# Attention rounds of the loop take 48 places instead of 64

## The reference, cut to what matters

```python
M = Bc * Nc                                     # 16384 nodes
h = (x_flat @ W_gat).reshape(M, HEADS, NUM_EXPERTS)
src = jnp.concatenate([edge_index[0], loops])   # 524288 edges, then one loop per node
dst = jnp.concatenate([edge_index[1], loops])
e = leaky_relu(a_src[src] + a_dst[dst], negative_slope=0.2)
e_max = jax.ops.segment_max(e, dst, num_segments=M)
ee = jnp.exp(e - e_max[dst])
denom = jax.ops.segment_sum(ee, dst, num_segments=M)
msg = h[src] * (ee / (denom[dst] + 1e-16))[:, :, None]
agg = jax.ops.segment_sum(msg, dst, num_segments=M)
...
'edge_index': jax.random.randint(ks[6], (2, N_EDGES), 0, B * N, jnp.int32)   # B * N = 32768
```

## Time and profile before

| what | value |
|---|---|
| median of 3 runs | 4333.23 us (4332.97 to 4335.96) |
| the profiled execution's own time | 4334.45 us |
| its span in the trace | 4332.5 us |
| busy: TensorE, VectorE, ScalarE, GpSimd | 68%, 70%, 36%, 31% |
| attention stage | about 2419 to 4140 us |
| turns in it | 20 (1280 gathers of L1481 at 64 a turn) |

### The profile page before, as it was taken

The page is one execution under the profiler, slowest core; times in us unless marked ns, Lnnn a source line. Parts: engine busy times, 40 slices in busy tenths (PEclk is TensorE's granted clock), DMA queues, the critical chain, the costliest instruction groups (busy, mean ns, idle before and its releaser), DMA issues. The chain is left out here.

```text
span 4332.5 us, 30277 instructions
## 1 busy us (share of the span) xinstructions
PE 2940.0 (68%) x9220; PEld 1488.6 (34%) x9220; DVE 3027.5 (70%) x4723; ACT 1553.3 (36%) x2238; POOL 1345.7 (31%) x1414
## 2 busy tenths in 40 slices
PE   6888897999999998998657235545554553554019
PEld 2333343343444443433234122322232332322019
DVE  8999668787888786987664546655654664665575
ACT  2222235444445454445453123323222322332117
POOL 0000000000000000001111577777777777777600
PEclk8888998999999999999768567666776776776559
DMA  4211322454545454548556212111111211111237
GB/s 152 76 64 54 112 93 79 128 176 140 174 150 172 141 179 139 187 143 272 168 178 225 33 29 51 37 37 44 47 37 44 47 37 40 31 18 18 23 134 287
DMA packets 341083, 454.19 MB, mean 105 GB/s; under 512 B 82749, under 2 KB 256712, under 8 KB 332090
## 3 DMA queue, kind: packets, MB, share of 16 engines
q1 hardware_dynamic: 289290, 389.20, 27.8%
q0 software_dynamic: 51632, 63.07, 7.7%
HBM read 340.70 MB, written 111.42 MB: 104 GB/s over the span
## 5 line engine op out<-in xcount | busy, mean ns | idle before, releaser
L1481 POOL DMA_INDIRECT got<-scratch_tab,src_at x1280 | 1224.0, 956 | 390.3 <-issue 378.7
L687 PE MATMUL in_ps<-tokens,w_in 128*128 128x512 f32 x2048 | 937.1, 610 | 4.4 <-issue 4.4
L1435 PE MATMUL hid_ps<-tokens,w 128*128 128x512 f32 x512 | 321.7, 762 | 823.0 <-ACT hid L1663 800.9
L614 POOL MEMSET tokens<- 1x128 int32 x1 | 0.2, 195 | 1923.0 <-DVE tokens L1069 1923.0
L687 PEld LDWEIGHTS in_ps<-tokens,w_in 128*128 128x128 f32 x2048 | 393.7, 196 | 484.8 <-issue 484.8
L704 PE MATMUL out_ps<-w_out,act 128*128 128x512 f32 x1024 | 478.8, 611 | 1.7 <-DMA w_out<-in_m_WoutT 1.7
L1068 DVE TENSOR_TENSOR tokens<-tokens 128x1024 f32<-128x1024 f32 x380 | 465.0, 1224 | 9.1 <-ACT tokens L852 8.0
L1069 DVE TENSOR_TENSOR tokens<-tokens 128x1024 f32<-128x1024 f32 x380 | 464.6, 1223 | 0.0
L1435 PEld LDWEIGHTS hid_ps<-tokens,w 128*128 128x128 f32 x512 | 111.4, 241 | 919.4 <-ACT hid L1663 810.7
L1588 DVE TENSOR_TENSOR hold<-by_value,is_loop 128x256 f32<-128x256 f32 x20 | 8.5, 426 | 581.7 <-ACT by_value L1674 581.7
L1674 ACT ACTIVATE by_value<-got 128x1536 f32<-128x1536 f32 x20 | 80.5, 4027 | 733.5 <-DMA got<-scratch_tab,src_at 733.5
(11 more groups left out here) (270 smaller groups left out, 4086.3 us busy)
## 6 DMA issues: line engine op xcount, KB each, us to landing
w_out<-in_m_WoutT SPq DMA_DIRECT2D x256, 512.0 KB, 4.6
w_in<-in_m_WinT SPq DMA_DIRECT2D x128, 512.0 KB, 4.0
scratch_y<-ys SPq DMA_DIRECT2D x25, 1024.0 KB, 4.0
got<-scratch_tab,src_at POOLq DMA_INDIRECT x1280, 2.4
tokens<-scratch_xt SPq DMA_DIRECT2D x8, 2048.0 KB, 9.4
scratch_sz<-zst SPq DMA_DIRECT2D x64, 256.0 KB, 5.0
gz<-scratch_sz SPq DMA_DIRECT2D x64, 256.0 KB, 5.0
tokens<-scratch_y SPq DMA_DIRECT2D x16, 1024.0 KB, 8.4
```

The source lines that it names most:

```text
L687: last = t_.matmul(in_ps[:, z, :], w_in[:, n % WIN, k, :], xT[:, s % 2, k, :], start=(k == 0), stop=(k == KC - 1))
L1435: last = t.matmul(hid_ps[:, f], w1[:, e, f * P:(f + 1) * P], tokens[:, g * QW:(g + 1) * QW], start=True, stop=True)
L1481: g.indirect_dma_start(got[:, y, t, :], None, tab_d[:, :], bass.IndirectOffsetOnAxis(ap=src_at[:, y, t:t + 1], axis=0))\
```

## The change

In the turns of the loop (18 and 19, and more if lists are longer) a turn takes FD = 48 places. The tiles stay 64 wide, and so do all of VectorE's and ScalarE's operations on them; the places 48 to 63 are marked as edges without effect. The carried state is read from column 48 there, at the end of `compute` rather than at the start of the next. The number of rounds of the loop is computed for 96 places a round. Three tiles that were written first by the moved copies are cleared once by GpSimd.

```diff
@@ -46,6 +46,9 @@
 FR = 64
 LOG_FR = 6
 LOG_2FR = 7
+FD = 48
+LOG_GROUP = 5
+THIRD = 21846
 ROW = H16 + 2 * HEADS
 TR = 256
 SUMS = HEADS * (EXP + 1)
@@ -1300,11 +1303,12 @@
                         ck(v.tensor_tensor(len_f[:, 1], ends[:, 2 * P:3 * P], ends[:, P:2 * P], ALU.subtract))
                         ck(v.tensor_scalar(len_f[:, 1], len_f[:, 1], float(-P), None, ALU.add))
                         ck(v.tensor_reduce(len_max, len_f.rearrange("x o p -> x (o p)"), AX.X, ALU.max))
-                        ck(v.tensor_scalar(slots_i, len_max, float(P + 1 + 2 * FR - 1), None, ALU.add))
-                        ck(v.tensor_scalar(slots_i, slots_i, LOG_2FR, None, ALU.logical_shift_right))
-                        ck(v.tensor_copy(len_max, slots_i))
-                        ck(v.tensor_scalar(rounds_i[:], len_max, float(PAIRS + 1), float(PAIRS), ALU.max,
-                                           ALU.subtract))
+                        ck(v.tensor_scalar(len_max, len_max, float(2 * FD - 1 + P + 1 - 2 * FR * PAIRS), float(2 * FD),
+                                           ALU.add, ALU.max))
+                        ck(v.tensor_copy(slots_i, len_max))
+                        ck(v.tensor_scalar(slots_i, slots_i, LOG_GROUP, None, ALU.logical_shift_right))
+                        ck(v.tensor_scalar(slots_i, slots_i, THIRD, None, ALU.mult))
+                        ck(v.tensor_scalar(rounds_i[:], slots_i, 16, None, ALU.logical_shift_right))
                         v.sem_inc(s_rnd, 1)
                         v.wait_ge(s_tw, 48)
                         for n in range(2):
@@ -1402,7 +1406,7 @@
 
 
             def rounds(eng):
-                return eng.value_load(rounds_i[0:1, 0:1], min_val=1, max_val=((NE + P + 2 * FR) >> LOG_2FR) - PAIRS)
+                return eng.value_load(rounds_i[0:1, 0:1], min_val=1, max_val=(NE + P + 2 * FD) // (2 * FD))
 
             @block.sync
             def _(sp):
@@ -1476,8 +1480,8 @@
                     g.indirect_dma_start(b_k[:, y], None, sorted_d[:, :],
                                          bass.IndirectOffsetOnAxis(ap=b_at[:, 0:1], axis=0)).then_inc(s_last, 16)
 
-                def gather(y):
-                    for t in range(FR):
+                def gather(y, n):
+                    for t in range(n):
                         g.indirect_dma_start(got[:, y, t, :], None, tab_d[:, :],
                                              bass.IndirectOffsetOnAxis(ap=src_at[:, y, t:t + 1], axis=0))\
                             .then_inc(s_got[y], 16)
@@ -1494,6 +1498,9 @@
                 g.memset(a_dst[:], 0.0)
                 g.memset(sink[:], -BIG)
                 g.memset(peak[:], 0.0)
+                g.memset(logit[:], 0.0)
+                g.memset(add[:], 0.0)
+                g.memset(hold1[:], 0.0)
                 g.memset(one_f[:], 1.0)
                 g.memset(run[:], 0.0)
                 g.memset(sums[:, 1], 0.0).then_inc(s_block, 1)
@@ -1507,7 +1514,7 @@
                         load_keys()
                         if not first:
                             load_last(1 - y)
-                        gather(y)
+                        gather(y, FR if first else FD)
                         g.wait_ge(s_block, 1)
                         g.sem_clear(s_block)
                         append(1 - y)
@@ -1523,7 +1530,7 @@
 
             @block.vector
             def _(v):
-                def merge(ck, r, y, last_on):
+                def merge(ck, r, y, last_on, width):
 
                     v.wait_ge(s_key, 16 * r + 16)
                     v.tensor_copy(lo_at[:, y], next_lo[:])
@@ -1542,9 +1549,11 @@
                     merged = merge_k[LOG_FR % 2][:].bitcast(I32)
                     v.tensor_scalar(src_at[:, y], merged, M - 1, None, ALU.bitwise_and)
                     ck(v.tensor_scalar(edge_i[:], merged, LOG_M, 1, ALU.logical_shift_right, ALU.bitwise_and))
-                    ck(v.tensor_copy(is_edge[:, y], edge_i[:]))
-                    ck(v.tensor_reduce(n_edge[:], is_edge[:, y], AX.X, ALU.add))
-                    v.tensor_scalar(next_lo[:], next_lo[:], n_edge[:, 0:1], float(FR), ALU.subtract, ALU.add)
+                    if width < FR:
+                        v.memset(is_edge[:, y, width:FR], 1.0)
+                    ck(v.tensor_copy(is_edge[:, y, 0:width], edge_i[:, 0:width]))
+                    ck(v.tensor_reduce(n_edge[:], is_edge[:, y, 0:width], AX.X, ALU.add))
+                    v.tensor_scalar(next_lo[:], next_lo[:], n_edge[:, 0:1], float(width), ALU.subtract, ALU.add)
                     ck(v.tensor_tensor(row_pos[:], row_pos[:], n_edge[:], ALU.add))
                     ck(v.tensor_copy(key_at[:], row_pos[:]))
                     if last_on:
@@ -1565,14 +1574,11 @@
                 def spread(x, n):
                     return x.unsqueeze(1).to_broadcast([P, n, FR])
 
-                def compute(ck, y):
+                def compute(ck, y, n):
 
                     row = by_value[:]
                     v.tensor_scalar(is_loop[:], is_edge[:, y], -1.0, 1.0, ALU.mult, ALU.add)
                     v.tensor_copy(hold0[:, :, 1:F1], spread(is_edge[:, y], HEADS))
-                    v.tensor_copy(logit[:, :, 0:1], peak[:, :, FR:F1])
-                    v.tensor_copy(add_r[:, :, 0:1], run[:, 0:SUMS, FR:F1])
-                    v.tensor_copy(hold1[:, :, 0:1], a_dst[:, :, FR:F1])
                     ck(v.tensor_tensor_scan(dist_f[:], one_f[:], is_edge[:, y], 0.0, ALU.mult, ALU.add))
                     v.tensor_scalar(sink[:, :, 1:F1], spread(is_loop[:], HEADS), -BIG, None, ALU.mult)
                     ck(v.tensor_tensor(dist[:], dist_f[:], is_loop[:], ALU.mult))
@@ -1613,13 +1619,16 @@
                                              .to_broadcast([P, OUTS, FR - d]), run[:, :, d:FR]), wait_apart)
                     ck(v.tensor_scalar(out_at[:, y], lo_at[:, y], bin_f[:, 0:1], sum_cap[:, 0:1], ALU.add, ALU.min))
                     v.sem_inc(s_packed, 1)
+                    v.tensor_copy(logit[:, :, 0:1], peak[:, :, n:n + 1])
+                    v.tensor_copy(add_r[:, :, 0:1], run[:, 0:SUMS, n:n + 1])
+                    ck(v.tensor_copy(hold1[:, :, 0:1], a_dst[:, :, n:n + 1]))
 
                 v.memset(keep_ps[:], 0.0)
                 v.wait_ge(s_gc, 1)
                 ck = Chain(v, s_mch)
                 v.tensor_copy(out_at[:, 1], sum_cap[:])
                 ck(v.tensor_copy(next_lo[:], bin_f[:]))
-                merge(ck, 0, 0, 0)
+                merge(ck, 0, 0, 0, FR)
                 v.wait_ge(s_last, 16)
                 v.wait_ge(s_gc, 2)
                 ck(v.tensor_scalar(b_mark, b_node[:], KEY_LAST, LAST_KEY, ALU.logical_shift_left, ALU.bitwise_or))
@@ -1630,13 +1639,14 @@
                     ck = Chain(v, s_mch)
                     for y in range(2):
                         if first:
-                            merge(ck, r + y + 1, 1 - y, FIRST_LAST if r + y + 1 == 2 * PAIRS else 0)
+                            turn = r + y + 1 == 2 * PAIRS
+                            merge(ck, r + y + 1, 1 - y, FIRST_LAST if turn else 0, FD if turn else FR)
                             count(ck, b_first[:, (r + y + 1) * FR:(r + y + 2) * FR])
                         else:
                             v.wait_ge(s_last, 16 * (r + y + 1) - 16 * (2 * PAIRS - 1))
-                            merge(ck, r + y + 1, 1 - y, FR)
+                            merge(ck, r + y + 1, 1 - y, FR, FD)
                             count(ck, b_k[:, 1 - y])
-                        compute(ck, y)
+                        compute(ck, y, FR if first else FD)
                     v.sem_clear(s_mch)
 
                 for i in range(PAIRS):
@@ -1667,10 +1677,10 @@
                 s.wait_ge(s_mw, 96)
                 s.wait_ge(s_gc, 2)
 
-                def pair(i, work=()):
+                def pair(i, work=(), got_before=0):
                     for y in range(2):
                         mine = list(work[y]) if work else []
-                        wait_apart(s, (s_got[y], 16 * FR * i + 16 * FR))
+                        wait_apart(s, (s_got[y], 16 * FR * i + 16 * FR if work else 16 * FD * i + got_before))
                         s.activation(by_value[:], got[:, y].rearrange("p f x -> p x f"), ACT.Copy).then_inc(s_turned, 1)
                         for n in mine[0:1]:
                             expert(n)
@@ -1700,7 +1710,7 @@
                     pair(i, [range(share[r], share[r + 1]) for r in (2 * i, 2 * i + 1)])
                 outcome(NQ_ALL * EXP - 1)
                 with s.Fori(0, rounds(s)) as i:
-                    pair(i + PAIRS)
+                    pair(i + PAIRS, (), 16 * FR * PAIRS + 16 * FD - 16 * FD * PAIRS)
 
 
         stage.close()
```

## The result

The changed kernel takes 4294.91 us, the median of 6 runs (4293.75 to 4297.71), against 4333.32 us for the kernel before in 6 runs: ratio 0.9909, 95% interval 0.9896 to 0.9922. The forecast was 4295 us, within 4291 to 4299. The execution that was profiled has a span of 4293.6 us.

The account below looks back on a forecast made before the run. GpSimd's issue of gathers, 1.25 us each, was taken to bound the attention stage. 4334.45 - 40.0 (gathers) + 1.5 (memsets) + 0.1 (count of rounds) = 4296.05, median 1.2 lower: 4295 us, range 4291 to 4299.

Parts of the forecast that it names:

- The number of turns: Attention stage's loop: longest list 1102 edges, below the 1120 that would need two rounds, so one round, turns 18 and 19.
- Gathers: Turns 18 and 19: 32 of 1280 gathers go, 16 a turn at 1.25 us, all on the path: 40.0 us less.
- Cover in turns 18 and 19: Time to spare behind GpSimd's gathers: ScalarE 6.8 us and VectorE 10.2 in turn 18, VectorE 9.0 in turn 19.
- another engine takes over: Rival, chance 0.05: VectorE's chain outgrows its 9.0 us cover in the last turn; 4300 us with 5 us beyond it.
- Memsets: Attention stage's start: GpSimd's three new clears hold VectorE's first merge operation, delaying all turns by 1.5 us (bounds 0 to 1.65).
- no hold: Rival, chance 0.22: at the stage's start the added clears cost nothing and gathers start where they did; 4293.3 us.
- Sum: Whole kernel: profiled 4334.45 us with all terms gives 4296.05; the runs' median lies 1.2 below, so 4294.8, say 4295 us.
- the way from the last gather to the next stage, 41.96 us, moves as a block: End of turn 19 to the next stage: tiles stay 64 wide, so nothing in the 41.96 us gets shorter; cost 0.

Follow-up runs that it names:

- the second pair of traces: Both kernels run again unaltered: the changed kernel 4297.09 us beside 4333.54 (ratio 0.9916); the kernel before, one run, 4333.87 us.

## Why the prediction was right

**The number of turns**: right; 1248 gathers and one round.

**Gathers**: right and of the right size, 20.1 us in each turn. That GpSimd's issue sets the length of a turn, on a chip with the usual time and at 48 places and more, was shown both ways, by 32 fewer and by 32 more.

**Cover in turns 18 and 19**: right. VectorE's predicted 9.0 us to spare in turn 19 were 9.33 and 8.21 in two traces, its 10.2 in turn 18 were 10.39 and 10.30. ScalarE's 6.8 were 10.5 and 6.6, since its expert work ends earlier in some executions. The rival that another engine takes over is refuted at 48 places, where all this cover was left over, and true at 40 and at 32 gathers, which go beyond it.

**Memsets**: right; +1.5 was predicted, the longer hold is 1.70 and the first gather 1.64 us later. The rival "no hold" is refuted. The Trainium skill's rule in "SBUF — State Buffer", section "SBUF: two separate sides" (of GpSimd's operations and certain kinds of VectorE's, the first to start on the shared port pair keeps it for its whole instruction, the other fully blocks), gives the direction; the trace goes beyond it. VectorE's operation started at 2422.30, beside the end of the clear of `run`, and was let in only behind the two clears of `sums` that followed, not behind the one that it met.

**Sum**: right within 0.1 us, and that closeness is luck. The step that failed is "the way from the last gather to the next stage, 41.96 us, moves as a block". It grew by 3.5 us: 2.86 through the DRAIN, which the change made longer, and 0.67 through the landing of the last gathers, which the second pair of traces does not repeat (3.4 and 3.5 us). In two sets of runs the changed kernel came 38.4 and 36.5 us below the kernel before beside it, where the terms as measured give -40.2 + 1.6 + 2.9 = -35.7; the rest, 1 to 3 us, is no larger than the scatter of the stages.

## What to carry to other kernels

A queue's idle time ahead of a wait is slack only if the waited-for work does not itself depend on that queue: here GpSimd's 5.00 us did not take up one microsecond of added clears. When work is cut from the engine that bounds a loop, write down every other engine's time to spare in each turn; the smallest is where the next cut stops paying in full, and it holds for the following experiments too. And a path "that moves as a block" across the end of a loop or a stage should be checked in the trace, since its end can change with the loop's code.

## What the hardware showed unexpectedly

- GpSimd's DRAIN at the end of the stage takes 5.692, 8.550, 3.732 or 3.078 us for 64, 48, 40 or 32 gathers a turn of the loop, the same to the nanosecond in each trace of a kind (one trace only for 32), with one round or two, and with 32 more gathers outside the loop.
- An operation of VectorE (the first merge operation, 128x64) waited until the last of several clears that GpSimd ran one behind the other, up to 4.79 us for one that takes 0.31, while VectorE's own clears beside GpSimd's were not held.
- One table row read by nearly all partitions raised the DMA share at 10 GB/s from 0.07 or 0.08 to between 0.18 and 0.31, and in one execution to 0.82. The issue still set the pace there at 1.25 us.
- On one chip the kernel before took 5027.5 us and the changed one 4950.7 (ratio 0.987, 0.983 to 0.991). Its trace has the usual first stage, the gathers still 1.25 us apart, but written turns of 113.7 us in the mean. The change took 77 us off there, twice the usual, which I cannot explain either. The waits there, the changed kernel, 2500 to 4500 us:

```profile
ACT ys L1665 <- remote: 991.8, 41, 47.7
...
POOL scratch_sums L1490 <- ACTq L1702: 531.2, 16, 39.9
```

GpSimd waits at its append for ScalarE, and ScalarE for something that the trace does not name. TensorE and VectorE have gaps of up to 38.1 and 43.7 us there as well that the trace puts down to no other engine. The cause was not tested and stays open.
